# Second expert loop: outputs of the leading 2048 tokens loaded, summed and stored beside the last blocks

## What is computed

```
x = x + 0.5 * ffn(layernorm(x), router_w, gate_w, up_w, down_w)
x = x + attention(layernorm(x), W_qkv, W_out)     # 8 x 512 tokens, 16 heads of 64, causal, rotary
x = x + 0.5 * ffn(layernorm(x), router_w, gate_w, up_w, down_w)
ffn: logits = x @ router_w.T; the best 2 of 8 experts, softmax of their 2 logits as weights
     out = sum of weight * ((silu(x @ gate_w[e].T) * (x @ up_w[e].T)) @ down_w[e].T), F = 512
```

## Time and profile before

| | |
|---|---|
| median of three runs | 1350.76 us |
| the profiled execution | 1353.68 us, its span 1351.6 us |
| mean granted TensorE clock | 0.956 |
| PE busy | 1232.3 us (91%), 8148 matmuls |
| DVE busy | 934.7 us (69%), 2002 instructions |
| ACT busy | 785.9 us (58%) |
| POOL busy | 848.0 us (63%) |
| HBM read, written | 35.53 MB, 15.60 MB |

### The profile page before, as it was taken

How to read it: one execution, slowest core, us unless ns; L and a number is a source line. 1 busy time by engine, 2 the same in 40 slices (tenths; PEclk the granted TensorE clock), 3 DMA queues, 4 the chain that set the end, 5 groups by cost and what they waited for, 6 DMA issues and landing times. The chain is left out here.

```text
span 1351.6 us, 27022 instructions
## 1 busy us (share of the span) xinstructions
PE 1232.3 (91%) x8148; PEld 906.6 (67%) x8148; DVE 934.7 (69%) x2002; ACT 785.9 (58%) x2230; POOL 848.0 (63%) x911
## 2 busy tenths in 40 slices
PE   7699999938999999999999999999998879999990
PEld 6488888825666666666666666666665658888880
DVE  5675333337888888888888888888887577533335
ACT  5455665515665666666666656656556455555552
POOL 4267776516767668677667677676665336766652
PEclk8799999967999999999999999999999889999995
DMA  9311111112212222221212222222111521111116
GB/s 306 113 40 45 47 48 46 40 51 58 55 46 48 64 48 48 63 48 47 56 42 63 48 48 64 48 47 48 45 42 26 180 84 41 44 48 49 46 40 190
DMA packets 86473, 86.44 MB, mean 64 GB/s; under 512 B 10496, under 2 KB 77056, under 8 KB 85824
## 3 DMA queue, kind: packets, MB, share of 16 engines
q1 hardware_dynamic: 73024, 63.99, 17.7%
q0 software_dynamic: 9088, 18.63, 4.9%
q10 hardware_dynamic: 4224, 2.10, 0.5%
HBM read 35.53 MB, written 15.60 MB: 38 GB/s over the span
## 5 line engine op out<-in xcount | busy, mean ns | idle before, releaser
L1382 POOL TENSOR_SCALAR at_prob<-at_prob,at_rec 128x128 f32<-128x128 f32 (+3 forms) x256 | 315.6, 1237 | 216.1 <-DVE at_rec L1554 215.0
L1638 ACT ACTIVATE at_prob<-at_s,at_nb 128x128 f32<-128x128 f32 (+3 forms) x512 | 265.4, 527 | 50.5 <-DVE at_nb L1546 45.9
L1647 ACT ACTIVATE at_probT<-at_pt 128x128 f32<-128x128 f32 (+3 forms) x256 | 105.0, 437 | 230.1 <-PE at_pt L1477 230.1
L1000 DVE TENSOR_TENSOR f_hid<-f_b,f_silu 128x512 f32<-128x512 f32 x142 | 98.1, 691 | 170.0 <-PE f_b L886 146.9
L1546 DVE TENSOR_REDUCE at_nb<-at_s 128x2 f32<-128x256 f32 (+3 forms) x256 | 208.8, 816 | 8.0 <-PE at_s L1463 8.0
L844 POOL DMA_INDIRECT f_xb<-xn_dram,f_source x142 | 147.7, 1040 | 87.6 <-issue 40.5
L853 POOL DMA_INDIRECT ys_dram<-f_y,f_target x142 | 139.8, 985 | 93.8 <-issue 58.8
L1477 PE MATMUL at_pt<-ident,at_prob 128*128 128x128 f32 x1280 | 184.4, 275 | 1.8 <-DVE at_prob L1557 1.2
L1458 PE MATMUL at_s<-at_KT,at_QT 64*128 64x128 f32 (+3 forms) x1024 | 175.3, 461 | 5.0 <-DMA at_KT<-at_R 3.7
L1376 POOL TENSOR_TENSOR at_R<-at_turned 128x512 f32<-128x512 f32 x128 | 159.3, 1263 | 30.4 <-DVE at_turned L1540 30.4
L1540 DVE TENSOR_TENSOR at_turned<-at_pj,rope 128x1024 f32<-128x1024 f32 x122 | 148.9, 1221 | 40.3 <-PE at_pj L1424 40.3
(11 more groups left out here) (261 smaller groups left out, 2152.0 us busy)
## 6 DMA issues: line engine op xcount, KB each, us to landing
at_QT<-at_R SPq DMA_DIRECT2D x128, 128.0 KB, 2.4
at_KT<-at_R SPq DMA_DIRECT2D x128, 128.0 KB, 2.3
f_gate<-gate_t SPq DMA_DIRECT2D x16, 256.0 KB, 4.9
f_up<-up_t SPq DMA_DIRECT2D x16, 256.0 KB, 6.6
xn_dram<-f_xn SPq DMA_DIRECT2D x16, 256.0 KB, 4.4
f_down<-down_t SPq DMA_DIRECT2D x2, 2048.0 KB, 8.0
at_got<-ys_dram SPq DMA_DIRECT2D x16, 256.0 KB, 3.3
f_got<-ys_dram SPq DMA_DIRECT2D x16, 256.0 KB, 5.1
```

The source lines that it names most:

```text
L1382: pool.tensor_scalar(w, w, rec[:, q, 1:2], None, ALU.mult).then_inc(probB_ready, 1)
L1638: act.activation(prob[q][:, h, :], s_bank[q % 2][:, h, 0:n], ACT.Exp, bias=nb[:, q, h:h + 1], scale=1.0, accum_out=sums[:, q, h:h + 1]).th ...
```

## The change

In both stages `gaps` is called per half of the tokens: for the leading ones at the end of the preparing block, for the others at j = 1. Their Exp (`odds`) stands at the head of ACT's loop program and after it; the weights (`shares`) at j = 20 and after the loop. In f2, SP waits in the loop until the scatters of blocks 0 to 38 have landed, loads the outputs of groups 0 to 3 into four new tiles (8 loads of 256 KB), and stores each group once DVE has added it. DVE adds two tiles of one expert in each of the iterations 47 to 62, between L994 and L1000 (`sum_leading`). The closing block keeps groups 4 to 7, with a semaphore for each; POOL and ACT have group 6 there, DVE groups 4, 5 and 7.

```diff
--- before.py
+++ after.py
@@ -326,9 +326,25 @@
-    def gaps(self, dve):
-        dve.tensor_tensor(self.wts[:, 0, :], self.best[:, 1, :], self.best[:, 0, :], ALU.subtract
+    def gaps(self, dve, r):
+        tiles = slice(self.tiles[r].start, self.tiles[r].stop)
+        dve.tensor_tensor(self.wts[:, 0, tiles], self.best[:, 1, tiles], self.best[:, 0, tiles], ALU.subtract
                           ).then_inc(self.gap_ready, 1)
+    def odds(self, act, r, ready):
+        tiles = slice(self.tiles[r].start, self.tiles[r].stop)
+        act.wait_ge(self.gap_ready, r + 1)
+        act.activation(self.wts[:, 1, tiles], self.wts[:, 0, tiles], ACT.Exp).then_inc(ready, 1)
+    def shares(self, dve, r, ready):
+        wts, link = self.wts, self.link
+        tiles = slice(self.tiles[r].start, self.tiles[r].stop)
+        dve.wait_ge(ready, r + 1)
+        link(dve.tensor_scalar(wts[:, 2, tiles], wts[:, 1, tiles], 1.0, None, ALU.add))
+        link(dve.reciprocal(wts[:, 2, tiles], wts[:, 2, tiles]))
+        link(dve.tensor_scalar(wts[:, 2, tiles], wts[:, 2, tiles], 0.5, None, ALU.mult))
+        link(dve.tensor_tensor(wts[:, 3, tiles], wts[:, 2, tiles], wts[:, 1, tiles], ALU.mult))
@@ -658,6 +674,7 @@
                     routing.sources(dve, 0)
+                    routing.gaps(dve, 0)
@@ -818,6 +835,13 @@
+        SCATTERED = routing.most + 5
+        def scattered(sp):
+            for k in range(AHEAD):
+                sp.wait_ge(y_out[k], 16 * ((routing.most - k + AHEAD - 1) // AHEAD))
         def has(j, d):
@@ -826,7 +850,31 @@
+        if out is not None:
+            lead_got = [sb(f"lead_got{g}", [P, 2, 4, P], ctx=work) for g in range(LEAD_GROUPS)]
+            lead_in = [sem(f"lead_in{g}") for g in range(LEAD_GROUPS)]
+            lead_added = sem("lead_added")
+            lead_stored = sem("lead_stored")
+            SUMMED = {SCATTERED + 3 + m: m for m in range(4 * LEAD_GROUPS)}
         with nc.Block() as block:
+            if out is not None:
+                @block.sync
+                def _(sp):
+                    scattered(sp)
+                    for g in range(LEAD_GROUPS):
+                        for k in range(2):
+                            first = (k * NB + 4 * g) * P
+                            sp.dma_start(lead_got[g][:, k, :, :],
+                                         ys_dram[first:first + 4 * P, :].rearrange("(n p) d -> p n d", p=P)
+                                         ).then_inc(lead_in[g], 16)
+                    for g in range(LEAD_GROUPS):
+                        sp.wait_ge(lead_added, 8 * g + 8)
+                        sp.dma_start(out[4 * g * P:4 * (g + 1) * P, :].rearrange("(n p) d -> p n d", p=P),
+                                     X[:, 4 * g:4 * g + 4, :]).then_inc(lead_stored, 16)
+                    sp.wait_ge(lead_stored, 16 * LEAD_GROUPS)
@@ -968,6 +1016,7 @@
+                routing.odds(act, 0, exp_ready)
                 for j in range(-1, BLOCKS + 3):
@@ -976,8 +1025,7 @@
                         leading(SPLIT[j])
-                act.wait_ge(routing.gap_ready, 1)
-                act.activation(wts[:, 1, :], wts[:, 0, :], ACT.Exp).then_inc(exp_ready, 1)
+                routing.odds(act, 1, exp_ready)
@@ -993,6 +1041,9 @@
                                           ALU.subtract).then_inc(xlo_ready, 1)
+                    if out is not None and j in SUMMED:
+                        sum_leading(SUMMED[j])
                     if has(j, 0):
@@ -1008,7 +1059,7 @@
                         routing.both_of(dve, 1)
-                        routing.gaps(dve)
+                        routing.gaps(dve, 1)
                     if j == COUNT_AT:
@@ -1035,6 +1086,20 @@
                         routing.pack(dve, 1)
+                    if j == TAKE_AT + 5:
+                        routing.shares(dve, 0, exp_ready)
+                def sum_leading(m):
+                    g, k, half = m // 4, m // 2 % 2, m % 2
+                    dve.wait_ge(lead_in[g], 32)
+                    if k:
+                        dve.wait_ge(lead_added, 8 * g + 2 * half + 2)
+                    for t in (2 * half, 2 * half + 1):
+                        n = 4 * g + t
+                        dve.scalar_tensor_tensor(out=X[:, n, :], in0=lead_got[g][:, k, t, :],
+                                                 scalar=wts[:, 2 + k, n:n + 1], in1=X[:, n, :],
+                                                 op0=ALU.mult, op1=ALU.add).then_inc(lead_added, 1)
@@ -1055,20 +1120,17 @@
                     dve.wait_ge(all_lo, AT_PIECES)
-                dve.wait_ge(exp_ready, 1)
-                link(dve.tensor_scalar(wts[:, 2, :], wts[:, 1, :], 1.0, None, ALU.add))
-                link(dve.reciprocal(wts[:, 2, :], wts[:, 2, :]))
-                link(dve.tensor_scalar(wts[:, 2, :], wts[:, 2, :], 0.5, None, ALU.mult))
-                link(dve.tensor_tensor(wts[:, 3, :], wts[:, 2, :], wts[:, 1, :], ALU.mult))
+                routing.shares(dve, 1, exp_ready)
...
             return
-        by_pool = [g for g in range(GROUPS) if g % 8 in (1, 3, 6)]
-        by_dve = [g for g in range(GROUPS) if g not in by_pool]
-        got = [sb(f"got{g}", [P, 2, 4, P]) for g in range(GROUPS)]
-        got_in = [sem(f"got_in{h}") for h in range(GROUPS // 2)]
+        LATE = range(LEAD_GROUPS, GROUPS)
+        by_pool = [g for g in LATE if g % 4 == 2]
+        by_dve = [g for g in LATE if g not in by_pool]
+        got = {g: sb(f"got{g}", [P, 2, 4, P]) for g in LATE}
+        got_in = {g: sem(f"got_in{g}") for g in LATE}
         weighted = sem("weighted")
@@ -1077,12 +1139,12 @@
             def _(sp):
-                for g in range(GROUPS):
+                for g in LATE:
                     for k in range(2):
...
                                      ys_dram[first:first + 4 * P, :].rearrange("(n p) d -> p n d", p=P)
-                                     ).then_inc(got_in[g // 2], 16)
+                                     ).then_inc(got_in[g], 16)
@@ -1098,7 +1160,7 @@
                 for m, g in enumerate(by_dve):
-                    dve.wait_ge(got_in[g // 2], 64)
+                    dve.wait_ge(got_in[g], 32)
                     for k in range(2):
@@ -1112,20 +1174,20 @@
                 for g in by_pool:
-                    act.wait_ge(got_in[g // 2], 64)
+                    act.wait_ge(got_in[g], 32)
                     for k in range(2):
...
                                            scale=wts[:, 2 + k, n:n + 1]).then_inc(weighted, 1)
-                for g in range(GROUPS):
+                for g in LATE:
                     if g in by_pool:
...
                                   X[:, 4 * g:4 * g + 4, :]).then_inc(stored, 16)
-                act.wait_ge(stored, 16 * GROUPS)
+                act.wait_ge(stored, 16 * len(LATE))
```

## The result

The changed kernel took 1341.63 us in the median of four runs (1340.26 to 1343.06), the kernel before 1352.69 in four (1350.12 to 1356.05): ratio 0.9917, 95% interval 0.9898 to 0.9936. In a second comparison, six runs against eleven, it was 1342.94 against 1352.82, ratio 0.9929, 0.9912 to 0.9945. The forecast was 1341.0 us, 9.8 less than the 1350.76 that the first three runs of the kernel before had given.

What follows compares the result with a forecast made beforehand. PE bounds attention and both expert loops; the 26.5 us closing block runs without PE, so work moved into the loop shortens the kernel. -10.1 + 0.3 = -9.8 us against the 1350.76 median gives 1341.0, range 1336.5 to 1346.0.

Steps and rivals of the forecast that it cites:

- The closing block: End of the kernel: with only groups 4 to 7 left it ends at 1341.5, 10.1 us less; ends 8.8 and 11.9.
- DVE's group 7: Last DVE adds of the closing block: 2.27 us plus 0.3 and 1.03 for POOL's adds, 3.6 after the eighth load.
- the lower end of the term: Closing block: both POOL adds met in full (0.75 more) and a store 0.5 us late at ACT's queue, 8.8 less.
- The loop: Second expert loop: two adds, 0.62 us, fit DVE's 1.37 us wait before L1000; cost 0, upper end 0.27 per gather.
- the gather's sensitive part: Second loop: POOL's gather needs something DVE can hold at its start; adds starting 0.6 us later come after that point.
- The transfers in the loop: Second loop's loads and stores: cost 0; up to 3.5 us if a gather waits behind all that SP has issued.
- The start of both stages: Preparing blocks: an extra `gaps` op adds 0.15 us twice, +0.3; early Exp and `shares` at j = 20 cost 0.
- (1): Second loop: leading groups' loads hold up gathers, PE waits near j = 42 to 46; up to +3.5, 1344.5; chance 0.10.
- (2): Second loop: POOL stretches the adds, DVE bounds 16 blocks, each 0.82 us longer; net +3.3, 1354.1; chance 0.05.
- DVE's limit: Second loop: DVE is free for 1.86 us of every block before its own work is longer than the block.
- (3): Closing block bound by POOL's group 6, ACT's store queue or a full DVE-POOL collision; 2 us less gain, 1343.0; chance 0.13.
- (4): Second loop: SP's wait ends late and the sums stall the loop; within 3 us of before; chance 0.04.

## Why the prediction was right

**The closing block** (10.1 us less forecast, range 8.8 to 11.9): 9.5 in the one profile, 9.8 in the other (26.5 to 17.0 and 16.7), and 8.9 to 10.3 by all seven profiles of this closing block. The landings of groups 4, 5 and 7 came 3.58, 6.72 and 10.02 us after SP's first load, where 3.5, 6.6 and 10.1 had been read off before; these loads carry over. The term that was off is DVE's group 7: 3.6 us taken, 4.24 measured. Group 6 did not: it landed at 8.5 us and not at 7.7 (the sixth load took 5.9 us and not 5.1), so POOL's adds began with group 7 and not a microsecond ahead of it, and DVE met both in full. That was the lower end of the term.

**The loop** (0): 0. The adds took 0.61 us of the 1.37, gather and scatter did not grow, and the loop from its first transpose to the closing block was 217.8 us against 217.7. That the adds missed the gather's sensitive part was read from the earlier trace rows; with eight adds, which reach into both, gathers and scatters took up to 2.6 us. The adds themselves, each begun while a gather was running, were not stretched:

```profile
L1100 DVE SCALAR_TENSOR_TENSOR X<-f_lead_got,wts,X x32: 341/346/349, 1244.8 to 1287.7; 128x128 f32<-128x128 f32 x32
```

The Trainium skill (SBUF — State Buffer, Who interferes with whom) has the one that starts first block the other for its whole length; for POOL's adds in the closing block the trace agrees (4.24 us against 2.31); for adds begun while a gather runs it does not (349 ns at the most), while a gather or scatter begun beside eight queued adds was held (up to 2.6 us).

**The transfers in the loop** (0, up to 3.5): 0. The gathers landed after 5.6 us at the most in this profile (5.7 in the second, 6.4 in the kernel with eight adds), under the 7.8 that PE can wait. The upper end rested on a queue served in order, and the run with twice the data refutes it. The Trainium skill (DMA: Bandwidth & Descriptors, Queues, rings and completion order) has the engines take turns among queues packet by packet; the landings of 4.8 to 5.4 us beside 4 MB agree.

**The start of both stages** (+0.3): +0.2. `gaps` begins 0.09 us behind `sources` and ends 0.08 behind it; the next block begins 0.58 us after `sources` did, 0.50 before (1103.46 to 1103.96), and the same in the first stage. The 0.15 us taken for each op was an estimate; it was 0.08.

```profile
1101.54 0.18 DVE L502 TENSOR_SCALAR f_source<-f_token 128x25 int32<-128x25 f32 x1
1101.63 0.17 DVE L331 TENSOR_TENSOR wts<-f_best 128x16 f32<-128x16 f32 x1
1102.12 0.37 DVE L524 TENSOR_TENSOR f_past<-const_first_place,f_ends 128x200 f32<-128x200 f32 x1 [0.32 <-PEq L621]
```

The early Exp ran while ACT waited. `shares` at j = 20 ended at 1171.07 and the next L1042 began at 1171.10, 0.34 us later behind its L1051 than before; the transposes stayed 2.84 us apart (1169.76 and 1172.60), so it cost nothing.

**The rivals.** (1) fell with the gathers' landings. (2) fell: no add in the loop was stretched by POOL. Four more adds a block cost nothing, six more 1.5 us in all, and about half of that by the reverse, DVE's adds holding POOL's gathers until PE waited for one. DVE's limit was put too low, at 1.86 us instead of 2.03 (an estimate from the block with eight adds), because I summed durations of instructions that overlap. (3) is what came in part: 0.6 us less gain by the collision, not by ACT's queue or POOL. (4) fell: the sums waited for nothing.

So the sum would have been 9.5 - 0.2 = 9.3 us by the first profile, against 9.8. The medians moved by 11.1 and 9.9 us; the difference to 9.3 is within what the executions of one kernel differ by ahead of the closing block. That 1341.63 lies within 0.7 us of 1341.0 is in part luck: the forecast started from 1350.76, and with its fourth run the kernel before stands at 1352.69.

## What to carry to other kernels

A closing stage that only gathers, adds and stores can be read transfer by transfer: the landings of the loads that stay carry over to the new kernel, here mostly within 0.4 us (the sixth came 0.5 to 1.4 later), and DVE's work is then laid behind them. After such a cut look again for the bound: with half of the work gone it lay between the loads and DVE, so that moving or dropping POOL's share, or finer counts with POOL's share kept, gave 16.35 to 17.1 us, no shown difference from the 16.2 to 17.6 of the unchanged block, and only dropping it together with finer counts gave less, 15.3. A difference of 2 us between two profiles is first to be compared with the same kernel's second profile, stage by stage. And a filler test that loses time has to be read block by block: the loss with eight adds looked like DVE's, and began with a late gather.

## What the runs showed of the hardware

Beside SP's loads the gathers of POOL's queue landed in 4.4 to 6.4 us instead of 2.5 with 2 MB queued at SP (in seven profiles, where the trace has the landing), and in 4.8 to 5.4 with 4 MB.

Gathers and scatters begun beside a queue of eight DVE adds with two SBUF inputs took 1.0 to 2.6 us instead of 1.0, and the slow ones ended 0.84 to 0.87 us behind the last of the adds. No add begun while one of them was running was stretched.

One chip ran the kernel before in 1416.08 us (1412.93 to 1421.56), 4.7% over the other chips. The loss was in the expert loops, as the profiles of the variants there show: 70 blocks of the second loop took 231 to 234 us where they take 200.7, many of them 2.84 us and others up to 6.4. Such a place, in the kernel with all late groups at DVE:

```profile
1301.47 0.28 ACT L1003 ACTIVATE f_y<-f_b 128x128 f32<-128x128 f32 x1 [2.48 <-remote]
1301.64 0.59 ACT L1007 ACTIVATE f_silu<-f_b 128x512 f32<-128x512 f32 x1
1302.07 1.15 PE L951 MATMUL f_b<-f_down,f_hidT 128*128 x8 [0.93 <-ACT f_y L1003]
```

ACT stood for 2.5 us before an instruction whose input PE had long finished, and the trace names no engine of the core for it; PE then waited for ACT. The cause was not looked for. In the closing block that chip was as fast as the others (adds of 0.28 us, 16.35 us in all).
